# Gate and up as three fp16 products, last rounds reordered, last tile stored by halves

## The reference, cut to what matters

```
x = x + attention(layernorm(x))            # 32 heads, binary weights
x = x + xattn(layernorm(x), ctx)           # a recurrent read/write block, below
x = x + ffn(layernorm(x), lora)            # 1024x1024 kernel, bias, two adapters

xattn: h = attention part (16 heads of 16, causal, rotary), written into the state
       g_in, u_in = read(h)                # two outputs of 256, normalised, scaled, shifted
       gate = g_in @ ctx[0].T ; up = u_in @ ctx[1].T      # 256 -> 1024 each
       h = write(h, silu(gate) * up)
```

## Time and profile before

| | |
|---|---|
| median of 3 runs | 939.95 us (936.91 to 940.65) |
| the profiled execution | 940.52 us, its span 938.8 us |
| mean granted clock of TensorE | 0.93 |
| busy share of the span | PE 88%, DVE 70%, ACT 45%, POOL 33% |
| chain that ended last, share by engine | PE 65%, DVE 16%, ACT 7%, issue 4%, SPq 3%, DMA 3%, POOL 2% |
| in that chain by line | L2036 (gate and up) 6%, L2011 5%, L1972 4% |

### The profile page before, as it was taken

The page is one execution under the profiler, slowest core; times in us unless marked ns, Lnnn a source line. Parts: engine busy times, 40 slices in busy tenths (PEclk is TensorE's granted clock), DMA queues, the critical chain, the costliest instruction groups (busy, mean ns, idle before and its releaser), DMA issues.

```text
span 938.8 us, 14942 instructions
## 1 busy us (share of the span) xinstructions
PE 827.4 (88%) x5530; PEld 439.4 (47%) x5530; DVE 658.8 (70%) x1381; ACT 420.3 (45%) x820; POOL 307.1 (33%) x297
## 2 busy tenths in 40 slices
PE   4899689999999999899977688868799999999977
PEld 2675233333333333366655223236665666656633
DVE  7875457888888986577875766434678778779661
ACT  4465415777777778024433356533342332332310
POOL 2000004676677678210010235432242232231210
PEclk9899899999999999999996668768799999999997
DMA  9664622232322232202236231110001101001011
GB/s 344 222 227 135 182 65 89 67 106 64 98 79 77 89 93 72 79 23 57 70 86 244 95 107 43 48 46 13 1 1 46 23 24 45 14 30 34 8 39 45
DMA packets 75626, 75.79 MB, mean 81 GB/s; under 512 B 37493, under 2 KB 63877, under 8 KB 74918
## 3 DMA queue, kind: packets, MB, share of 16 engines
q1 hardware_dynamic: 74998, 68.77, 23.9%
q10 hardware_dynamic: 560, 6.12, 1.6%
HBM read 53.56 MB, written 21.04 MB: 79 GB/s over the span
## 4 chain that ended last, share of the span: by engine, by line
PE 65%; DVE 16%; ACT 7%; issue 4%; SPq 3%; DMA 3%; POOL 2%; POOLq 0%; DVEq 0%; ACTq 0%; PEldq 0%
PE psum L1648 7%; PE psum L2036 6%; PE psum L2011 5%; PE psum L1730 5%; PE psum L1781 5%; DVE m_neg L1278 4%; PE psum L1972 4%; PE psum L1838 4%; PE psum L1845 4%; PE psum L1770 4%; PE psum L1791 3%; PE psum L1938 3%; PE psum L1916 2%; SPq L539 2%; PE psum L2024 2%
## 5 line engine op out<-in xcount | busy, mean ns | idle before, releaser
L1278 DVE TENSOR_REDUCE m_neg<-psum 128x1 f32<-128x512 f32 x256 | 165.5, 682 | 35.9 <-PE psum L1730 33.9
L915 ACT ACTIVATE region_x<-psum 128x512 f32<-128x512 f32 x256 | 142.7, 596 | 56.0 <-PE psum L1770 54.5
L682 POOL TENSOR_TENSOR region_p<-region_x 128x2048 f32<-128x2048 f32 x32 | 145.2, 4537 | 38.9 <-ACT region_x L915 24.9
L1730 PE MATMUL psum<-ops 96*128 96x512 f16 x256 | 96.7, 386 | 14.0 <-DMA ops<-q_scr 9.5
L1770 PE MATMUL psum<-ops 98*128 98x512 f16 x256 | 95.5, 381 | 0.9 <-ACT region_x L915 0.8
L1648 PE MATMUL psum<-region_x,region_w 128*128 128x512 f16 x320 | 76.8, 397 | 3.0 <-ACT region_w L853 3.0
L1730 PEld LDWEIGHTS psum<-ops 96*128 96x128 f16 x256 | 24.7, 97 | 95.9 <-DVE m_neg L1278 69.9
L2036 PE MATMUL psum<-ynT,region_w 128*128 128x128 f32 x512 | 63.6, 289 | 6.3 <-ACT ynT L1062 6.3
L1781 PE MATMUL psum<-region_x,v_g 128*32 128x512 f32 x512 | 67.8, 604 | 0.0
L2036 PEld LDWEIGHTS psum<-ynT,region_w 128*128 128x128 f32 x512 | 62.1, 204 | 9.9 <-ACT ynT L1062 9.9
L1838 PE MATMUL psum<-sign_o_all,region_a 128*128 128x512 f16 x256 | 58.5, 379 | 3.9 <-DVE region_p L1361 2.8
(11 more groups left out here) (240 smaller groups left out, 1482.0 us busy)
## 6 DMA issues: line engine op xcount, KB each, us to landing
ops<-q_scr SPq DMA_DIRECT2D x48, 128.0 KB, 2.7
region_a<-in_x SPq DMA_DIRECT2D x8, 512.0 KB, 7.8
region_a<-in_w_q SPq DMA_DIRECT2D x8, 512.0 KB, 6.6
region_w<-in_w_o SPq DMA_DIRECT2D x8, 512.0 KB, 4.1
region_w<-in_kern SPq DMA_DIRECT2D x16, 256.0 KB, 3.1
kern_scr<-region_w SPq DMA_DIRECT2D x32, 128.0 KB, 1.9
region_p<-in_x SPq DMA_DIRECT2D x8, 512.0 KB, 3.8
region_a<-kern_scr ACTq DMA_DIRECT2D x1, 4096.0 KB
```

What stands on the lines that cost most here:

```text
L682: pool.tensor_tensor(pair_sum[:, n], prob_a[:, 2 * n], prob_a[:, 2 * n + 1], ALU.add).then_inc(pair_ready, 1)
L915: act.activation(prob_a[:, kt, j, :], psum[:, (0, 4, 5)[(16 * i + n) % 3], :], ACT.Exp, scale=A_SCALE).then_inc(p_ready, 1)
L1278: dve.tensor_reduce(m_neg[:, i % 3, n:n + 1], psum[:, 1 + (16 * i + n) % 3, :], AX_X, ALU.max, negate=True).then_inc(s_max, 1)
L1730: pe.matmul(psum[:, 1 + (16 * i + n) % 3, :], qa_op[u][0:A_MAX, j, qt * P:(qt + 1) * P], k_op[u][0:A_MAX, :], start=True, stop=True).then_ ...
```

## The change

It has five parts.

1. Gate and up are computed as three fp16 products instead of one fp32 product: high weights by high tile, low weights by high tile, high weights by low tile, all summed in PSUM, 96 products of 128x128 by 128 columns instead of 32. Weights are scaled by `F_GAIN` = 64, which tanh's scale and the last factor take back.
2. The weights are split once, during cross attention rounds 2 to 5: ScalarE makes the high half, VectorE the low half, each in eight pieces of 128x512 (`CTX_TILES`), into parts of `ops` that are free by then and over the weights already split.
3. ScalarE writes the tile twice from PSUM, first as fp16 (`y2_hi`), then as fp32 (`ynT`); GpSimd's new `read_lo` makes the low half `y2_lo` from both, ahead of `write_h` in the rounds, and ahead of the whole `write` in the prologue. In the rounds all high products stand before all low ones; in the prologue gate is finished before up begins.
4. In round 8, ScalarE does `log_part(1)` and `decays(1)` ahead of the copy of the adapters' rows.
5. In round 9 the adapter product of the first half stands before `dense_hi(1)`, and the last tile is finished and stored in two halves of 512 columns. The semaphores `l_step` and `l_rstd` are merged into `ln_step` and `ln_rstd`.

```diff
+        _ctx = [ops[:, XI * 2 * S:(XI + 2) * 2 * S], ctx_parts[:, 0, :].bitcast(F16), ops[:, (XI + 2) * 2 * S:(XI + 4) * 2 * S], ctx_parts[:, 1, :].bitcast(F16)]
+        ctx_hi, ctx_lo = ([c[:, n * M:(n + 1) * M] for c in _ctx] for n in range(2))
+        y2_hi, y2_lo = (t[:].rearrange("p (c n) -> p c n", c=4) for t in (hi_st, lo_st))
+        CTX_TILES = {(i + 2, n): (i, n // 8) for i in range(4) for n in (3, 11)}
...
-            for i in (NT - 2, NT - 1):
-                store_out(i)
-            sp.wait_ge(out_stored, 16 * NT + 16)
+            store_out(NT - 2)
+            for h in range(2):
+                sp.wait_ge(out_ready, NT + 1 + h)
+                sp.dma_start(out[T - P:T, h * 512:(h + 1) * 512], out_t[:, h * 512:(h + 1) * 512]).then_inc(out_stored, 16)
+            sp.wait_ge(out_stored, 16 * NT + 32)
...
+            def read_lo(i):
+                pool.wait_ge(y2T_ready, 8 * i + 8)
+                pool.wait_ge(gu_mm, 2 * i)
+                pool.tensor_tensor(y2_lo, ynT[:, 0:4, :], y2_hi, ALU.subtract).then_inc(y2_lo_ready, 1)
...
             read_root_2(0)
+            read_lo(0)
             write(0, 1, h_in)
             attended(2)
             read_root_2(1)
+            read_lo(1)
             write(1, 0, h_0)
...
-                write(1, i - 1, h_mid[(i - 1) % 2])
+                write_a(1, i - 1, a3)
+                if i < NT:
+                    read_lo(i)
+                write_h(1, i - 1, h3, a3, wr)
...
+            def split_ctx_hi(c, h):
+                if (c, h) == (0, 0):
+                    act.wait_ge(xw_loaded, 16 * 6)
+                if h == 0 and c % 2 == 0:
+                    act.wait_ge(xst_mm, 16 * (c + 2))
+                if c % 2 == 1:
+                    act.wait_ge(ctx_lo_ready, 2 * (c // 2) + 2)
+                act.activation(ctx_hi[c][:, h * 512:(h + 1) * 512], ctx_parts[:, c, h * 512:(h + 1) * 512], ACT.Copy, scale=F_GAIN).then_inc(ctx_hi_ready, 1)
...
                 for n, (kt, j) in enumerate(X_PROB_TILES):
+                    if (i, n) in CTX_TILES:
+                        split_ctx_hi(*CTX_TILES[i, n])
...
-            def read_turned(i):
+            def read_turned(i, *forms):
                 act.wait_ge(y2T_mm, i + 1)
-                for n in range(4):
-                    act.activation(ynT[:, n, :], psum[:, 7, n * P:(n + 1) * P], ACT.Identity,
-                                   scale=cols[:, g2 + n:g2 + n + 1], bias=cols[:, b2 + n:b2 + n + 1]).then_inc(y2T_ready, 1)
+                for to in forms:
+                    for n in range(4):
+                        act.activation(to[:, n, :], psum[:, 7, n * P:(n + 1) * P], ACT.Identity,
+                                       scale=cols[:, g2 + n:g2 + n + 1], bias=cols[:, b2 + n:b2 + n + 1]).then_inc(y2T_ready, 1)
...
                 if first:
                     decays(0, i)
+                if second and not first:
+                    log_part(1, i - 1)
+                    decays(1, i - 1)
                 if dense:
                     act.wait_ge(axT_mm, i - 1)
...
+            def split_ctx_lo(c, h):
+                dve.wait_ge(ctx_hi_ready, 2 * c + h + 1)
+                part = slice(h * 512, (h + 1) * 512)
+                dve.scalar_tensor_tensor(ctx_lo[c][:, part], ctx_parts[:, c, part], F_GAIN, ctx_hi[c][:, part],
+                                         ALU.mult, ALU.subtract).then_inc(ctx_lo_ready, 1)
...
+                    if (i, n - 4) in CTX_TILES:
+                        split_ctx_lo(*CTX_TILES[i, n - 4])
...
-            finish(NT - 1)
+            dve.wait_ge(out_stored, 16 * NT)
+            for h in range(2):
+                half = slice(h * 512, (h + 1) * 512)
+                dve.wait_ge(f_mm, NT + 1 + h)
+                dve.scalar_tensor_tensor(out_t[:, half], psum[:, 4 + h, :], 1.0 / F_GAIN, x1[:, NT - 1, half], ALU.mult, ALU.add).then_inc(out_ready, 1)
...
+            def gate_product(n, f, k, w, y, bank, start, stop):
+                at = (bank, 6)[n] + f // 4
+                return pe.matmul(psum[:, at, (f % 4) * P:(f % 4 + 1) * P], w[2 * n + k][:, f * P:(f + 1) * P], y[:, 2 * n + k, :], start=start, stop=stop)
+
+            def gate_up_hi(i, bank, parts=range(2)):
+                pe.wait_ge(y2T_ready, 8 * i + 4)
+
+                for n in parts:
+                    for f in range(KC):
+                        if (n, f) == (1, KC // 2):
+                            pe.wait_ge(y2T_ready, 8 * i + 8)
+                        for k in range(2):
+                            gate_product(n, f, k, ctx_hi, y2_hi, bank, f % 4 == 0 and k == 0, False)
+                            gate_product(n, f, k, ctx_lo, y2_hi, bank, False, False)
+
+            def gate_up_lo(i, bank, parts=range(2)):
+                pe.wait_ge(y2_lo_ready, i + 1)
+                for n in parts:
...
+                            mm = gate_product(n, f, k, ctx_hi, y2_lo, bank, False, f % 4 == 3 and k == 1)
                     mm.then_inc(gu_mm, 1)
...
                 if dense:
                     pe.wait_ge(axT_ready, i - 1)
+                    if last:
+                        adapters(0).then_inc(f_mm, 1)
                     dense_hi(1, range(KC))
...
-                    gate_up(i, 0)
+                    gate_up_hi(i, 0)
+                    gate_up_lo(i, 0)
```

More of the change, by code:

```diff
@@ L1089, in round_ @@
                     turned(h2T, 6, h2T_ready)
-                if second:
+                if second and first:
                     log_part(1, i - 1)
                 if first:
-                    read_turned(i)
-                if second:
+                    read_turned(i, y2_hi, ynT)
+                if second and first:
                     decays(1, i - 1)
@@ L1101, in _ @@
             low_first(1)
-            read_turned(0)
+            read_turned(0, y2_hi, ynT)
             log_part(0, 1)
@@ L1110, in _ @@
             log_part(1, 0)
-            read_turned(1)
+            read_turned(1, y2_hi, ynT)
             decays(1, 0)
@@ L1370, in residual @@
                 for h in range(2):
[L1371 to L1377, removed]
+                    dve.bn_stats(st[:, 0, h, :], x1[:, i, h * 512:(h + 1) * 512]).then_inc(ln_step, 1)
+                dve.wait_ge(ln_step, 4 * NT + 5 * i + 2)
+                dve.bn_aggr(mv[:, 0, :], st[:, 0]).then_inc(ln_step, 1)
+                dve.wait_ge(ln_step, 4 * NT + 5 * i + 3)
+                dve.tensor_copy(mvs[:, 2 * i:2 * i + 2], mv[:, 0, :]).then_inc(ln_step, 1)
+                dve.tensor_scalar(ves[:], mv[:, 0, 1:2], LN_EPS, None, ALU.add).then_inc(ln_step, 1)
+                dve.wait_ge(ln_rstd, NT + i + 1)
                 if i > 0:
@@ L2029, in turn_read, with adapters @@
                 turn(7, yn, 4, y2T_mm)
-            def gate_up(i, bank):
-                pe.wait_ge(y2T_ready, 4 * i + 4)
-                for n, at in ((0, bank), (1, 6)):
+            def gate_product(n, f, k, w, y, bank, start, stop):
[13 more added lines that the diff above has]
+                for n in parts:
                     for f in range(KC):
                         for k in range(2):
-                            mm = pe.matmul(psum[:, at + f // 4, (f % 4) * P:(f % 4 + 1) * P], ctx_w[:, n, k, f * P:(f + 1) * P], ynT[:, 2 * n + k, :],
-                                           start=(k == 0), stop=(k == 1))
+                            mm = gate_product(n, f, k, ctx_hi, y2_lo, bank, False, f % 4 == 3 and k == 1)
                     mm.then_inc(gu_mm, 1)
+            def adapters(h):
+                return pe.matmul(psum[:, 4 + h, :], axT, lora_bt[0:R2 + 1, h * 512:(h + 1) * 512], start=False, stop=True)
             def round_(i, u, first, second, dense, done):
+                last = not first and not second
                 if first:
@@ L2087, in round_ @@
                 if first:
-                    gate_up(i, 0)
+                    gate_up_hi(i, 0)
+                    gate_up_lo(i, 0)
                 if dense:
                     dense_lo(1, range(5, KC))
-                    for h in range(2):
-                        mm = pe.matmul(psum[:, 4 + h, :], axT, lora_bt[0:R2 + 1, h * 512:(h + 1) * 512], start=False, stop=True)
-                    mm.then_inc(f_mm, 1)
+                    if not last:
+                        adapters(0)
+                    adapters(1).then_inc(f_mm, 1)
             pe.wait_ge(xo_copied, XI)
@@ L2106, in _ @@
             turn_read(0)
-            gate_up(0, 2)
+            for n in range(2):
+                gate_up_hi(0, 2, (n,))
+                gate_up_lo(0, 2, (n,))
             pe.wait_ge(mlp_ready, 4)
@@ L2114, in _ @@
             turn_read(1)
-            gate_up(1, 0)
+            for n in range(2):
+                gate_up_hi(1, 0, (n,))
+                gate_up_lo(1, 0, (n,))
             run_rounds(pe, round_)
```

15 lines of the change are left out of this document (9 added, 6 removed).

## The result

Over 20 executions each, the median is 932.62 us (929.0 to 939.93) against 938.64 us for the kernel before; the ratio is 0.9942, 95% interval 0.992 to 0.9963. The forecast was 930.5 us, with a range of 923 to 938. By the medians the kernel is 6.0 us faster. The two profiled executions differ by more: spans of 929.7 and 938.8 us, 9.1 apart. The profiled execution of the kernel after (931.4 us) lies 1.2 us under its kernel's median, that of the kernel before (940.52) 1.9 us above its own.

What follows compares the result with a forecast made beforehand. TensorE was taken to set the steady rounds, with VectorE close behind. Terms +3 +1.4 +2.2 +0.8 -9.35 -1.13 -3.15 -2.0 -1.1 sum to -9.3 us from 940.52, giving 931.2, stated as 930.5 for the median; range 923 to 938.

Steps and rivals of the forecast that it cites:

- Rate of the fp16 products: Gate and up, steady round: 96 products 0.056 us apart, 5.38 us of issue against 7.25, so 1.87 us less.
- Rival (a): Gate and up: fp16 products bound by their weight loads, 0.10 us each, giving 956 us; chance 0.09.
- Rounds: Tiles 2 to 7: five rounds save 1.87 us each, 9.35 in all; the sixth, limited by VectorE, saves 1.13.
- Rival (b): Rounds: VectorE becomes the bound, L1522 is 1.6 us late, 0.9 us a round arrive, giving 935.5 us; chance 0.15.
- Prologue: Tiles 0 and 1, where TensorE is not the limit: a loss of +1.4, +2.2 and +0.8 us.
- The order: Prologue, tile 0: four more ScalarE reads stand before the logarithm VectorE waits for, +1.4 us.
- the clock behind tile 0: Prologue: TensorE idles 4.8 us after tile 0's gate products, so the products behind run slower, +2.2 us (0 to 3).
- tile 1: Prologue: `write_a` queued on GpSimd behind `read_lo` delays TensorE's next products, +0.8 us (0.3 to 1.6).
- Splits in attention: Cross attention rounds 2 to 5: ScalarE's copies cost nothing, VectorE's differences 0.8 us a round, +3 us (0 to 6.4).
- The hoist: Round 8: logarithm moved ahead of the adapters' row copy, VectorE's wait of 4.15 us becomes about 1.0, -3.15 us.
- The clock in the last round: Last turn and products behind it: idle time shrinks to about 2 us, slow stretch may go, -2.0 us (0 to -3.2).
- The halves: Last tile: shorter last VectorE step (1.22 to about 0.7 us) and smaller last store (about 0.6 less), -1.1 us.

Runs made afterwards that it cites:

- the fillers: Kernel after plus products nobody reads: 22 behind tile 0's gate and up, ratio 0.9926; or 9 and 4 around the last turn, 0.9883, both to the kernel before.
- Doubling: Kernel after with each of VectorE's eight differences of the weights computed twice in a row; ratio 1.0009 to the kernel before.
- the halves alone: Kernel before with only the last tile's halves and the early adapter product; ratio 0.9985 to the kernel before.
- Gate and up alone: Kernel after with the earlier round 8 logarithm and the last tile's halves taken back; ratio 0.9978 to the kernel before.

## Why the prediction was right, and where it was off

The time was 2.1 us above the forecast, and the mechanisms were mostly the ones named. Some of that nearness is luck. The forecast was worked out as 9.3 us less than one profiled execution. The two profiles differ by 9.1, but the medians by 6.0 only, and the kernel before came out at 938.64 us where the forecast started from 939.95. And two terms of the sum are off with opposite signs: in the pair of profiles the splits cost 3.2 us less than forecast, and the clock of the last round gave 2.3 us less.

- **Rate of the fp16 products:** right. 96 records take 5.53 us in a round, (5.53-0.22)/95 = 0.056 us apart, with loads of 0.098 us hidden. Rival (a) fell, and with it the 81 ns of the Trainium skill ("TensorE: Matmul & The Clock Gate", "Back-to-back issue gap"): the trace does not agree with it, here in 96 pairs in a row.
- **Rounds:** right step by step. L1561 (then L1522) ends 6.05 us behind the first gate product, forecast 6.1; L1610 7.18, forecast 7.2; period 34.07, forecast 34.1. Five rounds gave 9.38 us (9.35), tile 7's 1.12 (1.13). Rival (b) fell. Left out was that a round's clock can slip: 0.9 us in the mean.
- **Prologue:** right in size. The order cost 1.6 us (forecast 1.4), the clock behind tile 0 2.6 in this profile and 2.2 in the mean of six (2.2), tile 1 0.7 (0.8) to its next products. The clock's term is confirmed by the fillers. The two of order are confirmed in part: turning the order back gave 0.72 of tile 0's 1.63 us, since `read_lo` then ran beside VectorE, and 2.14 us to tile 1's next products, more than the 0.70 lost there.
- **Splits in attention:** the sign and the place were right, the size was too large: 1.8 us in the mean against 3 (1.4 with all eight pieces). The single profile would have said nothing at all. The mechanism, VectorE's differences as waits of TensorE, is not what the profiles show: the time stands there as a lower clock. Doubling shows that there is no slack: another 4.5 us of VectorE work cost 8 us of this stretch in one profile, of an execution 5 us above its kernel's median, and 6 us of time by the two ratios.
- **The hoist:** right, -2.98 against -3.15. VectorE's wait went to 1.08.
- **The clock in the last round:** the step that failed. I wrote that the idle time before the last turn shrinks to about 2 us "so the slow stretch behind it may go", and took -2.0. The idle time did shrink to 2.13 us, but the clock fell in all five kernels with these last rounds. Against the halves alone (22.51 us from the last turn to the end) they take 22.28 in the mean, so the term is -0.2, and +0.3 in the profile of after. In three of them the turn itself still runs at the low clock. In after it went from 1.97 to 1.09 us, and the dense product behind it from 5.04 to 5.54. What was missed is that TensorE idles a second time, behind the turn, for 1.2 to 2.1 us: the adapter products start 2.95 us behind the turn's start in after, held by the load of their rows, where 2.27 was possible. The fillers show that the clock was to be had: 1.9 us in the mean, and the load 1.02.
- **The halves:** -1.12, forecast -1.1.

Put the means of the profiles in place of the single pair, and the change is worth -9.1 + 2.0 (attention: the mean of seven, and not the cheapest) + 0.9 (rounds) + 0.1 (prologue) - 0.5 (the last round) = -6.6 us, near the medians' -6.0. This is no proof of the single terms. The kernel before has only three profiles for its attention, and that its profiled execution lies 1.9 us above its median is not explained.

## What to carry to other kernels

Splitting an fp32 product into three fp16 ones pays by the issue pitch (0.113 x 2 per fp32 product against 3 x 0.056), but only where TensorE sets the pace. In a prologue that VectorE paces, the same edit is pure cost: shorter TensorE work there lengthened the idle time (1.38 to 5.22 us), and the clock was low behind it. When a stall before a product is shortened, look at the whole idle pattern around it and at each load that was hidden in the stall. And one pair of profiles can flatter a change in every stage at once: the stage times of a few variants, side by side, gave the scatter that the pair hid.

## What the runs showed of the hardware

- Products whose results are thrown away bought time: 4.91 us of them, wholly inside an idle gap, took 2.6 us off the 16 products behind them in one pair of profiles and 2.2 in the mean, and 3.1 us of them around the last turn took off 1.9 in the mean. The granted clock was 1.00 behind the first of these and 0.50 without.
- Behind the same idle time of 2.1 us the last turn took 1.09 us in two profiles and 1.97 in three.
- With the doubled VectorE work three rounds of attention took 36.39 us instead of 30.51 (one profile each) while TensorE's busy time rose from 27.74 to 32.87: most of the loss stands in the profile as a busy engine at a granted clock of 0.64, and not as its waits. Gate and up alone, without the doubling, had 33.24 us at 0.65.
- GpSimd and VectorE exclude one another in the prologue too: a VectorE step of 0.41 us took 1.41 beside `read_lo`'s 1.16. The Trainium skill ("SBUF — State Buffer", section "SBUF: two separate sides") says that whichever of the two starts first keeps the shared ports for its whole instruction. The rows agree to about 0.1 us: `read_lo` had started 0.03 us earlier, and VectorE's step ended 0.28 us behind it, where the whole step behind it would be 0.41.
